# The order of groups in two routings of a mixture of experts: dense branches of three groups moved to the end, ranks and places moved forward

## The reference

```python
x = x + attention_a(layernorm(x))      # linear attention, 8 heads
x = x + ffn(layernorm(x))              # mixture of experts
x = x + attention_b(layernorm(x))      # causal softmax attention
x = x + ffn(layernorm(x))              # mixture of experts, same weights
```

```python
xn = normalise(x) * gamma + beta
abel_out = gelu(xn @ abel_w + abel_b)                 # the dense branch
logits = xn @ moe_gate_w + moe_gate_b                 # 8 experts
topw, topi = top_k(logits, 2); topw = softmax(topw)
moe_out = sum over the two experts of topw * (gelu(xn @ ew1[e] + eb1[e]) @ ew2[e] + eb2[e])
moe_out = moe_out @ expm(gens[0]) @ expm(gens[1]) @ expm(gens[2])
gate = sigmoid(concat(abel_out, moe_out) @ gc_w + gc_b)
return x + abel_out * (1 - gate) + moe_out * gate
```

## Time and profile before

| | |
|---|---|
| median of 3 runs | 1418.49 us (1414.6 to 1419.76) |
| the profiled execution | 1422.55 us |
| its span | 1420.9 us, 26058 instructions |
| PE busy | 1180.7 us (83%) |
| DVE busy | 862.8 us (61%) |
| ACT busy | 495.4 us (35%) |
| POOL busy | 411.6 us (29%) |
| mean DMA rate | 114 GB/s |

### The profile page before, as it was taken

One profiled execution on the slowest core, in us unless ns is written; L12 is line 12 of the kernel. 1 busy time (PEld: TensorE's weight loads), 2 busy tenths in 40 slices (PEclk: granted clock), 3 DMA queues, 4 the chain that ended last, 5 costly groups with the idle time before them and its releaser, 6 DMA issues.

```text
span 1420.9 us, 26058 instructions
## 1 busy us (share of the span) xinstructions
PE 1180.7 (83%) x7280; PEld 1022.1 (72%) x7281; DVE 862.8 (61%) x2756; ACT 495.4 (35%) x967; POOL 411.6 (29%) x480
## 2 busy tenths in 40 slices
PE   6796876955599999992699998999883799999958
PEld 5664555854488989992588987888772688998947
DVE  6435766744456666665676658766536456666646
ACT  1111551332244444441233333343342334444435
POOL 3001101566134444441000000104454244444420
PEclk9897995877899999996899999999896799999989
DMA  9400231446474333335011011001157663343357
GB/s 288 145 0 7 83 119 52 153 149 215 152 237 120 90 91 89 91 87 208 0 46 45 1 45 46 1 1 56 71 217 244 198 226 103 105 135 103 106 173 249
DMA packets 75727, 161.73 MB, mean 114 GB/s; under 512 B 11302, under 2 KB 36594, under 8 KB 75642
## 3 DMA queue, kind: packets, MB, share of 16 engines
q1 hardware_dynamic: 55082, 105.45, 21.5%
q0 software_dynamic: 19776, 54.45, 12.5%
q10 hardware_dynamic: 784, 0.79, 0.2%
HBM read 88.92 MB, written 71.73 MB: 113 GB/s over the span
## 4 chain that ended last, share of the span: by engine, by line
PE 52%; issue 12%; DVE 6%; DMA 3%; ACT 3%; another core or an unknown queue 3%; POOL 3%; POOLq 1%; SPq 1%; DVEq 0%; ACTq 0%
PE bank L2077 15%; PE bank L1621 6%; PE bank L1622 6%; PE bank L1490 6%; PE bank L1623 6%; PE bank L1647 3%; PE bank L1700 2%; DMA xh<-slots_in 2%; PE bank L2135 2%; POOL xh L1301 2%; PE bank L1630 2%; PE bank L1533 1%; PE bank L186 1%; POOLq L1300 1%
## 5 line engine op out<-in xcount | busy, mean ns | idle before, releaser
L1621 PE MATMUL bank<-ew,rows 128*128 x852 | 298.4, 350 | 4.3 <-DVE rows L1175 2.6
L1622 PE MATMUL bank<-low_in,rows 128*128 x852 | 273.3, 321 | 0.0
L1623 PE MATMUL bank<-ew,rows 128*128 x852 | 272.8, 320 | 0.0
L1312 POOL DMA_INDIRECT results<-xh x142 | 141.8, 998 | 295.7 <-DVE xh L1203 277.5
L1621 PEld LDWEIGHTS bank<-ew,rows 128*128 128x128 f32 x852 | 161.8, 190 | 15.3 <-issue 8.2
L1623 PEld LDWEIGHTS bank<-ew,rows 128*128 128x128 f32 x852 | 161.4, 189 | 12.2
L1622 PEld LDWEIGHTS bank<-low_in,rows 128*128 128x128 f32 x852 | 162.5, 191 | 6.0
L1457 ACT ACTIVATE xh<-bank 128x512 f32<-128x512 f32 x142 | 85.0, 599 | 219.4 <-PE bank L1623 219.4
L1212 DVE TENSOR_TENSOR rows<-bank,rows 128x512 fp32r<-128x512 f32 x142 | 98.3, 692 | 96.1 <-ACT rows L198 82.1
L1291 POOL DMA_INDIRECT slots_in<-xh,work x120 | 117.1, 976 | 101.2 <-DVE work L1071 67.6
L634 POOL TENSOR_TENSOR work<-work,mhalf 128x8 f32<-128x8 f32 (+1 forms) x22 | 38.7, 1760 | 332.7 <-DVE work L627 332.6
(11 more groups left out here) (334 smaller groups left out, 2037.5 us busy)
## 6 DMA issues: line engine op xcount, KB each, us to landing
xh<-slots_in POOLq DMA_DIRECT2D x142, 129.0 KB
low_in<-low SPq DMA_DIRECT2D x32, 512.0 KB
xh<-results SPq DMA_DIRECT2D x14, 1032.0 KB, 5.2
residual<-xs SPq DMA_DIRECT2D x16, 512.0 KB
dense<-ab SPq DMA_DIRECT2D x16, 512.0 KB
xs<-residual SPq DMA_DIRECT2D x16, 512.0 KB
ab<-dense SPq DMA_DIRECT2D x9, 512.0 KB, 9.3
xs<-in_L_attn_a_x_dram SPq DMA_DIRECT2D x4, 1024.0 KB
```

Of the source, the lines that this page charges most:

```text
L1312: pool.indirect_dma_start(out=yg, out_offset=bass.IndirectOffsetOnAxis(ap=back[j % RING], axis=0), in_=yr[j % RING], in_offset=None).then_ ...
L1621: pe.matmul(o, hi, f32r(high(c)), start=(c == 0), stop=False)
L1622: pe.matmul(o, hi, f32r(low(c)), start=False, stop=False)
L1623: last = pe.matmul(o, lo, f32r(high(c)), start=False, stop=(stop and c == chunks[-1]))
```

## The change

In the second mixture the order becomes 3, 4, 5, 6, 7, 0, 1, 2, so that the five groups that are still to be routed come first, and the three whose routing is done get their turn and dense product last. PE's product for the totals moves from behind the loop to step 5. SP fetches no weights among the spills; those of experts 0 and 1 come after the paddings. DVE takes three dense gates, not four, ahead of the tables. In the first mixture, `located_first` is true for groups 0 to 3 (before: for group 0 alone): PE does the ranks of groups 1 to 3 ahead of the dense product of the step, and DVE does `locate` right behind `choose`, ahead of `normalise(g + 2)` and `statistics(g + 4)`.

```diff
-            ORDER = [3, 0, 4, 1, 5, 2, 6, 7] if r == 1 else list(range(NG))
+            ORDER = [*range(EARLY_GROUPS, NG), *range(EARLY_GROUPS)]
...
+            def located_first(g):
+
+                return g == EARLY_GROUPS or (r == 0 and g < NG // 2)
...
-                LATE = {NG - 4: (0,), NG - 3: (1,), NG - 2: (2, 3)} if r == 0 else {NG - 3: (0,), NG - 2: (1,), NG - 1: (2, 3)}
+                LATE = {NG - 4: (0,), NG - 3: (1,), NG - 2: (2, 3)} if r == 0 else {NG - 3: (0,), NG - 2: (1,), NG - 1: (2,)}
...
                 for g in range(EARLY_GROUPS, NG):
                     choose(v, g)
-                    if g == EARLY_GROUPS:
+                    if located_first(g):
                         locate(v, g)
                     if g + 2 < NG:
                         normalise(v, g + 2)
...
-                    if g > EARLY_GROUPS:
+                    if not located_first(g):
                         locate(v, g)
...
-                for p in range(NG // 2, NG):
+                for p in range(NG // 2 if r == 0 else NG // 2 - 1, NG):
                     dense_gate(ORDER[p])
...
                 def fetch_weights(e):
                     after(sp, low_ld, WEIGHTS * e)
 
-                    sp.wait_ge(spilled[e % 4], 32 * (e // 4 + 1 if r == 0 else 2))
+                    sp.wait_ge(spilled[step_of[e] % 4], 32 * (step_of[e] // 4 + 1 if r == 0 else 2))
...
                     spill(p)
-                    if 0 <= p - (3 if r == 0 else 5) < EARLY:
-                        fetch_weights(p - (3 if r == 0 else 5))
+                    if r == 0 and 0 <= p - 3 < EARLY:
+                        fetch_weights(p - 3)
...
                 for n in range(1, LATE_FOLDS):
                     store_fold(n)
+                for e in range(EARLY if r == 1 else 0):
+                    fetch_weights(e)
                 sp.wait_ge(x_ld[RING - 1], 16)
...
+                    if p == 1 or (chosen and located_first(chosen[0])):
+                        rank(pe, chosen.pop())
                     if p >= 2:
                         dense(p - 1)
-                    if p == 1:
-                        rank(pe, chosen.pop())
                     if routed:
                         route(ORDER[p])
                     if chosen:
...
                     if p == 1:
                         dense(0)
+                    if p == NG - EARLY_GROUPS and r == 1:
+                        total_rows()
```

More of the change, by code:

```diff
@@ L977, in mixture @@
             EARLY_GROUPS = 3 if r == 1 else 0
-            ORDER = [3, 0, 4, 1, 5, 2, 6, 7] if r == 1 else list(range(NG))
+            ORDER = [*range(EARLY_GROUPS, NG), *range(EARLY_GROUPS)]
             step_of = {g: p for p, g in enumerate(ORDER)}
-            assert all(step_of[g] < step_of[g + 4] for g in range(NG - 4))
             if r == 0:
@@ L1319, in spill @@
                     sp.wait_ge(res_ok, GT * (g + 1))
-                    sp.dma_start(xs_out[g], xs[:, tiles(g), :].rearrange("p t c -> p (t c)")).then_inc(spilled[g % 4], 16)
+                    sp.dma_start(xs_out[g], xs[:, tiles(g), :].rearrange("p t c -> p (t c)")).then_inc(spilled[p % 4], 16)
                     sp.wait_ge(gelu_ok, p + 1)
-                    sp.dma_start(ab_out[g], ab[:, tiles(g), :].rearrange("p t c -> p (t c)")).then_inc(spilled[g % 4], 16)
+                    sp.dma_start(ab_out[g], ab[:, tiles(g), :].rearrange("p t c -> p (t c)")).then_inc(spilled[p % 4], 16)
                 def fetch_weights(e):
                     after(sp, low_ld, WEIGHTS * e)
-                    sp.wait_ge(spilled[e % 4], 32 * (e // 4 + 1 if r == 0 else 2))
+                    sp.wait_ge(spilled[step_of[e] % 4], 32 * (step_of[e] // 4 + 1 if r == 0 else 2))
                     sp.wait_ge(zab_ok, GT * (step_of[e] + 1))
@@ L1568, in tensor, with total_rows @@
                     attend(2)
+                def total_rows():
+                    pe.wait_ge(run_ok, NG)
+                    pe.wait_ge(lg_ok, NG)
+                    pe.matmul(bank[:, 6, 0:E], onesb[:], run[NG % 2], start=True, stop=True).then_inc(rank_ps, 1)
                 chosen = []
@@ L1593, in tensor @@
                     turn_late(1)
-                pe.wait_ge(run_ok, NG)
-                pe.wait_ge(lg_ok, NG)
-                pe.matmul(bank[:, 6, 0:E], onesb[:], run[NG % 2], start=True, stop=True).then_inc(rank_ps, 1)
+                if r == 0:
+                    total_rows()
                 pe.wait_ge(xT_ok, NG)
```

## The result

The kernel after takes 1431.43 us, median of six runs (1429.68 to 1435.69); the kernel before took 1419.12 us (1414.6 to 1423.8) in the same series. The ratio is 1.0100 with an interval of 1.0083 to 1.0117, so the change costs 12.3 us between the medians (14 us by the ratio) where 7 us of gain were predicted. The profiled execution took 1435.69 us.

A forecast was written before the change was run, and what follows sets the result against it. Chains of waits in the two routings, in the second through SP, were taken to bound what the change touches. Second routing 9.8 us gained less first routing 3.0 gave 6.8 off 1418.5: 1411.5 us, range 1403 to 1427.

The forecast's parts named there:

- the last gelu stays at 1077.6: Second routing, PE: same products in any order, so the last gelu does not move; 0 us.
- The prediction's own sign of being wrong: Second routing: last gelu beyond 1085 us and PE gaps put down to issue while POOL runs.
- held signals: Rival: PE's signals arrive late during POOL's scatter runs; one 14.3 us hold gives 1426 us, tail to 1440; chance 0.20.
- The last spill: Second routing, SP: last spill waits for the gelu alone, issued about 1077.9 instead of 1085.37; 7.5 us gained.
- The padding: Second routing, SP: eight padding writes take 11 us instead of 14.28; 3.3 us gained, bounds 0 and 5.7.
- Behind the padding: Second routing: 7.9 us from padding to first expert product, for expert 0's weights and row path alike; change 0.
- Two loads more in the loop: Second expert loop: weights of experts 0 and partly 1 load beside the first tiles; 1.0 us lost.
- smooth routing: Rival: half of PE's idle 11 us in the second routing goes, last gelu 5 us sooner; 1404.5 us, chance 0.13.
- The sum of 9.8 us: Second routing's total gain: 7.5 (last spill) + 3.3 (padding) - 0 - 1.0 (extra loads).
- gains used up: Rival: slow padding, short holds and first-routing loss, or the scatters' landing, cancel the gain; 1419 us, chance 0.25.
- The credit given to SP's part alone: Second routing: weights leaving the queue ahead of the padding credited with 7.5 us (spill), then 3.3 us (padding).
- The first routing: New waits and later statistics delay POOL's roots by 2.6 us; 3.0 us lost, bounds 5.3 lost to 6.6 gained.

The follow-up runs named there:

- e3: Kernel before, group order kept, with only SP's part: second-routing weights of experts 0 and 1 fetched behind the paddings; 1369.95 us, ratio 1.0012 to before.
- e10: Kernel before with only the first routing's part of the change, repeated on another chip without held signals; ratio 1.002 to before.
- e9: Kernel before with only SP's part (weights of experts 0 and 1 behind the paddings), repeated on another chip without held signals; ratio 0.9987 to before.
- e1: Kernel before with only the first routing's part (ranks of groups 1 to 3 ahead of the dense product, places behind the choice); 1373.39 us, ratio 1.0032.
- e2: Kernel before with only the second routing's part (new order, weights behind paddings, totals early), on a chip without held signals; 1360.1 us, ratio 0.9934.
- e4: Kernel after, with at most two scatters under way in the second routing, on a chip without held signals; 1384.4 us, ratio 1.0114 to before.
- e11: Kernel after, with at most two scatters under way in the second routing, repeated on another chip without held signals; ratio 1.01 to before.
- e12: Kernel after, with POOL waiting for the last gelu before group 6's scatters in the second routing, chip without held signals; ratio 1.0057 to before.
- e5: Kernel before, unchanged, profiled on a chip with held signals; 1414.23 us (one run).
- e14: Kernel before with only SP's part (weights of experts 0 and 1 behind the paddings), on a chip with held signals; ratio 1.0 to before.
- e6: Kernel after, unchanged, timed again on a chip with held signals; 1431.19 us, ratio 1.0089 to before.
- e7: Kernel before with only the second routing's part of the change, on a chip with held signals; 1426.93 us, ratio 1.0057 to before.
- e13: Kernel after, unchanged, timed once more on another chip with held signals; 1433.98 us, ratio 1.0111 to before.
- e16: Kernel after, with POOL waiting for the last gelu before group 6's scatters in the second routing, chip with held signals; 1430.15 us, ratio 1.0096 to before.
- e8: Kernel after, with POOL waiting for the last gelu before group 5's scatters in the second routing, chip with held signals; 1428.1 us, ratio 1.0064 to before.
- e15: Kernel after, with at most two scatters under way in the second routing, on a chip with held signals; ratio 1.0055 to before.
- e18: Kernel before plus the second routing's part, scatters in pairs, at most four under way in both routings, chip with held signals; 1403.88 us, ratio 0.9925.

## Why the prediction was wrong

**The step that failed** is the first term of the second routing, "the last gelu stays at 1077.6". It summed PE's products, whose number doesn't change, and took their length and the waits between them as given. The stretch to the last gelu became 23.6 us longer: 16.0 us of idling and 7.6 us of products at a lower granted clock. In the profiles it goes by order and chip:

| first logits product of the second routing to the end of the last gelu | order of before | new order |
|---|---|---|
| chips without holds | 53.9, 53.9, 57.6, 57.7 us (e3, e10, e9, e1) | 56.5 to 56.8 us (e2, e4, e11, e12) |
| chips with holds | 65.8, 68.2, 68.4 us (before, e5, e14) | 89.0 to 89.4 us (after, e6, e7, e13) |

So without holds the step was right within 3 us, and with them it was wrong by 21 to 24. The prediction's own sign of being wrong came: the last gelu beyond 1085 us, with gaps of PE put down to issue. The rival "held signals" had the mechanism, the place (one run of scatters over groups 5 to 7 with the late dense products under it) and the direction; its chance of 0.20 and its price of one hold of 14.3 us were too small. The rows of before could have raised both: the prediction took from them that no wait in the second routing is as long as 14 us, but signals were late there already, by 19.1 us in five waits of ACT. The longest, from the timeline of ACT before:

```profile
1063.39 0.20 ACT L198 ACTIVATE work<-bank 128x32 f32<-128x32 f32 x1 [6.35 <-remote]
```

The two holds in the chain come to 17.0 us, and the result of 1431.4 lies between its 1426 and its 1440. The argument against it, that a hold starves POOL and so ends itself, failed: when the last dense products run, all ranks are done and POOL has 16 scatters in hand that need nothing of PE. That the change put just the products without a rank behind them under the scatters was in the diff; I should have asked what could still end the run.

**The last spill** (7.5 us sooner after its gelu) was right: 7.7. **The padding** was sized at 11 us and took 8.24, just under the 8.6 of its quick pace, with no scatter issued beside it any more. With scatters beside it, it takes 11.4 to 16.1 us on chips with holds (e16, e8, e5, before, e14) and 8.1 to 10.1 without (e1 to e3, e9, e10, e12); with at most two scatters under way it is 8.4 to 8.8 on either (e4, e11, e15). **Behind the padding**, 7.9 us was taken and 10.2 measured: the last padding lands after 3.18 us for 2.57, and from POOL's first fetch to PE's first tile it is 4.2 us (1120.20 to 1124.38) for 2.5 (1105.67 to 1108.17), with the weights of expert 0 in flight beside both. This second price goes with the weights in all profiles: 3.8 to 5.5 us in the eleven with weights in flight at the fetch, 2.5 in the nine without. The prediction had taken the row path as unchanged. Those weights took 7.8 us (1116.15 to 1123.91), in the predicted range. The Trainium skill, page "DMA: Bandwidth & Descriptors", section "Anatomy of one DMA — SWDGE (gpsimd) path", would give an estimate of 5.6 us, and the trace again does not agree; that fit of the Trainium skill is for single DMAs that GpSimd issues, and these are three of SP's. **Two loads more in the loop** (-1.0) didn't show: from the first expert product to the end it is 310.9 us before and 307.9 after, but such differences don't sort by the change: 307.0 to 310.9 in the four profiles with the weights ahead of the padding (before, e1, e5, e10), 307.2 to 311.2 in nine with them behind (after, e2, e3, e6 to e9, e13, e14).

**The rival "smooth routing"** set PE's busy time of the whole window (54.5 us) against 65.6 us of it; up to 1076.6 PE is busy 52.4 us, so the idle time was 13 us and not 11.

**The sum of 9.8 us** was measured as 9.1 on the chip without holds, but that is luck: it came about for another reason. There the scatters' landing sets the first tile in the order of before (e3, e9), as the rival "gains used up" said, and it is the order that brings them forward. The credit given to SP's part alone was wrong on every chip: 1.0012, 0.9987, 1.0.

**The first routing** was predicted at 3.0 us lost with roots 2.6 us late. Measured: 4.4 and 2.7 alone, 4.3 as the difference of the medians of e6 and e7, 5.4 in the profile after, a little beyond the bound of 5.3. The first roots are 1.9 us late with holds (before and after; e7 and e6) and 0.8 to 3.4 without. The mechanism, later roots, was right, and so was the direction; the size is good to a factor of two. With holds there is one thing more: the place now waits for the rank ahead of the statistics, and this signal is one of those that come late. Timeline of DVE, first routing, after:

```profile
296.69 0.19 DVE L1069 TENSOR_TENSOR work<-bank,ebase 128x32 f32<-128x32 f32 x1 [10.93 <-remote]
```

**Shown and only argued.** That scatters under way hold PE's products on some chips is shown by e8, which moves the scatters, and by e15, which limits them. Whether the number under way or the pace counts is open. Why they do so, and why some chips don't, is open; no run here looks inside the DMA engines or the semaphores.

## What to carry to other kernels

Count for a moved product not only its length but what runs beside it in the new place: a stretch with many indirect DMAs under way cost 21 to 24 us on chips with holds here and under 3 us on those without. Before trusting a gain of a per cent, time it on several chips, since the same edit was 0.66% faster on one and 0.57% slower on another. If indirect DMAs come in long runs, try a limit on how many are under way, and pick it by measurement: two freed PE and starved POOL, four in both routings came out 0.75% ahead on the one chip, with holds, on which they were tried.

## What the runs showed of the hardware

The chips met here differ by up to 50 us on this kernel, and nearly all of it lies in the two routings. Timeline of PE, the first tile of the first routing, before on its chip, then e9 on a chip without holds: 35.5 us apart. From the same logits product under the attention to the first tile of the second routing it is 155.7 us before (952.50 to 1108.17) and 141.5 in e9 (917.12 to 1058.65), 14.2 more; together 49.7 of the 51.1 us between the two spans.

```profile
390.09 0.41 PE L1630 MATMUL bank<-ident,xh 128*128 128x128 f32 x2 [0.73 <-issue]
```

```profile
354.57 0.41 PE L1632 MATMUL bank<-ident,xh 128*128 128x128 f32 x2 [0.73 <-ACT ew L198]
```

The scatters themselves finish late where signals are held. POOL's first fetch, behind the last scatter of the first routing, waits for their landing; timelines of POOL, before and e9:

```profile
372.57 0.59 POOL L1301 DMA_DIRECT2D xh<-slots_in  x1 [12.71 <-issue]
```

```profile
349.02 0.59 POOL L1301 DMA_DIRECT2D xh<-slots_in  x1 [3.87 <-issue]
```

In e18, with at most four under way on a chip with holds, this wait is 4.02 us. In all other profiles of chips with holds it is 11.6 to 13.2 us, in all of chips without 3.8 to 4.6. So a chip with holds falls behind with the scatters that POOL issues every 1.27 us, and while it is behind, others' signals are late as well. That the two have one cause is argued from their going together in these profiles, not shown.
